# Layer 2 of a four-layer mixture kernel: the next batch's first two up products moved ahead of this batch's last down product, and two DVE steps moved by one or more slots

## What is computed

```python
# conditioning: y = x @ W_base.T + b_base + low-rank expert part (rank 16 of each of 8 experts)
out = einsum('btc,oc->bto', x, W_base) + b_base
h = einsum('btc,erc->bter', x, As)
y = out + einsum('bter,eor,be->bto', h, Bs, w) * SCALING
# feed-forward on the better half of the tokens (k = 256 of 512), F = 1024
scores = einsum('bsd,d->bs', y, w_router)
top_scores, top_idx = top_k(scores, k)
weights = sigmoid(top_scores)
h = gelu(selected @ W1 + b1)
update = weights[:, :, None] * (h @ W2 + b2)      # added to the selected tokens, the others pass through
x = x + (y + scattered update)
```

## Time and profile before

| | |
|---|---|
| median of three executions | 1460.94 us |
| the profiled execution, its own time | 1467.98 us |
| its span, first to last instruction | 1465.3 us |
| PE busy | 1292.0 us, 88% of the span |
| DVE busy | 1017.1 us, 69% |
| POOL busy | 628.9 us, 43% |
| ACT busy | 573.3 us, 39% |
| mean granted TensorE clock | 0.926 of full speed |
| layer 2 from up(1, 0) to the last down product | 698.34 to 800.60 us of the span |

### The profile page before, as it was taken

One profiled execution on the slowest core, in us unless ns is written; L12 is line 12 of the kernel. 1 busy time (PEld: TensorE's weight loads), 2 busy tenths in 40 slices (PEclk: granted clock), 3 DMA queues, 4 the chain that ended last, 5 costly groups with the idle time before them and its releaser, 6 DMA issues.

```text
span 1465.3 us, 18770 instructions
## 1 busy us (share of the span) xinstructions
PE 1292.0 (88%) x6536; PEld 1093.1 (75%) x6536; DVE 1017.1 (69%) x1854; ACT 573.3 (39%) x960; POOL 628.9 (43%) x339
## 2 busy tenths in 40 slices
PE   5998999998992899838888999999899989996798
PEld 4898687897791799826677787877678777875687
DVE  8699777599662555546766433489748994799986
ACT  3401423303320688714445454434443344432242
POOL 4320115620015567573303462375445442565691
PEclk9899999899975899969999999999899999998799
DMA  6310002310007689851101647323213161232000
GB/s 193 145 37 15 29 19 82 132 29 1 0 15 254 206 274 315 264 172 43 44 0 35 223 169 250 127 73 126 111 50 109 50 244 65 73 122 101 0 1 29
DMA packets 45885, 154.96 MB, mean 106 GB/s; under 512 B 6992, under 2 KB 7776, under 8 KB 45664
## 3 DMA queue, kind: packets, MB, share of 16 engines
q1 hardware_dynamic: 38848, 136.08, 27.7%
q0 software_dynamic: 4608, 12.59, 2.6%
q10 hardware_dynamic: 2336, 5.11, 0.9%
HBM read 120.98 MB, written 32.77 MB: 105 GB/s over the span
## 4 chain that ended last, share of the span: by engine, by line
PE 57%; DVE 22%; issue 9%; POOL 5%; ACT 4%; DMA 2%; SPq 1%; DVEq 0%; ACTq 0%; POOLq 0%
PE bank L442 17%; PE bank L446 16%; PE bank L445 16%; DVE G L498 3%; DVE bank L2472 3%; DVE acc L2496 2%; DVE F L2496 2%; POOL w_lo L679 1%; POOL VW L498 1%; PE bank L1056 1%; PE bank L1228 1%; POOL xs L687 1%; PE bank L1373 1%; DVE acc L2628 1%; PE bank L928 1%
## 5 line engine op out<-in xcount | busy, mean ns | idle before, releaser
L442 PE MATMUL bank<-x_hi,w_hi 128*128 128x512 f32 (+1 forms) x560 | 218.6, 390 | 27.9 <-POOL w_lo L725 6.3
L445 PE MATMUL bank<-x_lo,w_hi 128*128 128x512 f32 (+1 forms) x560 | 212.6, 380 | 0.0
L446 PE MATMUL bank<-x_hi,w_lo 128*128 128x512 f32 (+1 forms) x560 | 212.2, 379 | 0.0
L725 POOL TENSOR_TENSOR w_lo<-raw,w_hi 128x1024 fp32r<-128x1024 f32 x36 | 89.4, 2482 | 196.1 <-ACT w_hi L1718 181.9
L442 PE MATMUL bank<-hid_hi,w_hi 128*128 128x512 f32 x328 | 133.3, 406 | 22.6 <-DVE hid_lo L2427 12.3
L442 PEld LDWEIGHTS bank<-x_hi,w_hi 128*128 128x128 f32 x560 | 110.2, 197 | 54.5 <-issue 18.5
L1819 ACT ACTIVATE hid_hi<-bank 128x512 fp32r<-128x512 f32 x96 | 57.6, 600 | 215.1 <-DVE bank L2472 215.1
L445 PE MATMUL bank<-hid_lo,w_hi 128*128 128x512 f32 x328 | 131.2, 400 | 0.0
L446 PE MATMUL bank<-hid_hi,w_lo 128*128 128x512 f32 x328 | 130.8, 399 | 0.0
L446 PEld LDWEIGHTS bank<-x_hi,w_lo 128*128 128x128 f32 x560 | 109.7, 196 | 19.2
L445 PEld LDWEIGHTS bank<-x_lo,w_hi 128*128 128x128 f32 x560 | 110.2, 197 | 17.8
(11 more groups left out here) (468 smaller groups left out, 3537.1 us busy)
## 6 DMA issues: line engine op xcount, KB each, us to landing
raw<-in_skill SPq DMA_DIRECT2D x32, 768.0 KB
raw<-in_l1e SPq DMA_DIRECT2D x20, 513.0 KB
base<-xs SPq DMA_DIRECT2D x38, 256.0 KB, 4.4
ys<-F SPq DMA_DIRECT2D x38, 256.0 KB, 4.8
VW<-in_l1e SPq DMA_DIRECT2D x18, 513.0 KB, 5.3
w_hi<-kept SPq DMA_DIRECT2D x12, 768.0 KB, 4.3
w_lo<-kept SPq DMA_DIRECT2D x12, 768.0 KB, 6.1
raw<-in_l0c SPq DMA_DIRECT2D x12, 512.0 KB
```

Source lines behind the costliest of these rows:

```text
L442: i = nc.tensor.matmul(out, sh, mh, start=first, stop=False)
L445: nc.tensor.matmul(out, sh, ml, start=False, stop=False)
L446: return nc.tensor.matmul(out, sl, mh, start=False, stop=last)
L725: nc.gpsimd.tensor_tensor(lo[:, UP3], src[:, UP3], hi[:, UP3].bitcast(F32), ALU.subtract).then_inc(w_up_ready.sem, 1)
```

## The change

On PE, up(b + 1, 0) and up(b + 1, 1) leave the head of the next batch: the first is issued ahead of `weights_of_tokens(b)`, the second between it and down(b, 7). On DVE, `add_ffn(b - 1)` moves from m = 0 to m = 1, and the four rank steps from m = 0, 1, 2, 3 to m = 0, 2, 3, 4. `x2_residue(b + 1)` stays at m = 4 and now stands ahead of a rank step. ACT, POOL and SP have the same instructions in the same order.

```diff
             for b in range(BATCH):
                 for m in range(8):
-                    l2_up(b, m)
+                    if b == 0 or m >= 2:
+                        l2_up(b, m)
                     if m >= 1:
                         l2_down(b, m - 1)
...
+                if b + 1 < BATCH:
+                    l2_up(b + 1, 0)
                 weights_of_tokens(b)
+                if b + 1 < BATCH:
+                    l2_up(b + 1, 1)
                 l2_down(b, 7)
...
+            RANK_SLOT = [0, 2, 3, 4]
             for b in range(BATCH):
                 u = b % 2
                 for m in range(8):
...
-                    if m == 0 and b > 0:
+                    if m == 1 and b > 0:
                         add_ffn(b - 1)
                     if m == 3 and b + 1 < BATCH:
                         add_experts(b + 1)
-                    if m < NT:
-                        rank_tokens(b, m)
+                    if m == 4 and b + 1 < BATCH:
+                        x2_residue(b + 1)
+                    if m in RANK_SLOT:
+                        rank_tokens(b, RANK_SLOT.index(m))
                     if m == 4:
-                        if b + 1 < BATCH:
-                            x2_residue(b + 1)
                         select_tokens(b)
```

## The result

| | before | after |
|---|---|---|
| median, five executions each | 1460.05 us | 1448.77 us |
| lowest and highest | 1458.51, 1464.66 | 1445.28, 1452.40 |
| the profiled execution, own time | 1467.98 us | 1452.24 us |
| its span | 1465.3 us | 1449.8 us |

The sign was right, the size was not. The execution behind the rows ahead of the prediction, 1467.98 us, is none of the five timed ones and lies above them all; the profiled one of after, 1452.24, is among its five. That will matter.

A forecast was written before the change was run, and what follows sets the result against it. PE, busy 88% of the span, was taken to bound the kernel, so only its idle time could pay. Batches 1, 2 and 3 gave 0 + 2.35 + 2.6 = 5.0 us: 1460.94 - 5.0 = 1456.0 us, range 1451.5 to 1460.5.

The forecast's parts named there:

- Batch 2: Layer 2, batch 2: gaps ahead of down(2, 0) and down(2, 1) go, transposes then wait for add_ffn(1); gives 2.35 us.
- 1.00 granted: Batch 2, PE's clock: no fall behind the 2.51 us gap, cited against the rival of a slower kernel.
- Batch 3: Layer 2, batch 3: down(3, 1) 3.4 us earlier, full clock, less a new collision; gives 2.5 to 2.6 us.
- the collision: Batch 3, slice 2: DVE's rank step 1 meets POOL's x_lo and stalls 1.9 us; without it batch 3 gives 4.2.
- batch 1 gives nothing: Layer 2, batch 1: PE's signal waits for gathers to land, so gelu of slice 3 stays at about 712.5; 0 us.
- Batch 1 gives too: Rival, chance 0.27: batch 1's late signal is fixed in length or moves with PE; 2.35 more, 7.3 us in all, 1453.6.
- Most is lost: Rival, chance 0.15: larger collision in batch 3, clock falls behind batch 1's new wait; 1 to 3 us remain, about 1459.
- Slower by the clock: Rival, chance 0.06: clock falls at new waits and layer 3's start cost 8 us against 5; about 1463.

The follow-up runs named there:

- before_paced: The kernel before, with POOL waiting after every three gathers of batches 2 and 3 until these have landed; ratio 0.9977 to the kernel before, 1458.37 us.
- before_third: The kernel before, unchanged, run again on a chip where it took 1467.58 us; ratio 1.0006.
- before_fourth: The kernel before, unchanged, run again on a chip where it took 1469.58 us; ratio 0.9977.
- before_again: The kernel before, unchanged, profiled a second time on a chip where it took 1468.59 us; ratio 0.9992.
- after_again: The changed kernel, unchanged, profiled a second time; ratio 0.9942 to the kernel before, which took 1468.59 us on that chip.
- after_fourth: The changed kernel, unchanged, on a chip where the kernel before took 1467.58 us; ratio 0.9926 to the kernel before.
- paced: The changed kernel, with POOL waiting after every three gathers of batches 2 and 3 until these have landed; ratio 0.9907 to the kernel before, 1446.47 us.
- paced_again: The changed kernel with gathers of batches 2 and 3 issued three at a time, on a chip where the kernel before took 1467.58 us; ratio 0.9910.
- all_together: The changed kernel plus gathers in threes, ACT's later rounding, and rank steps at slices 1, 2, 2, 4 (batch 0: 0, 2, 2, 4); 0.9848 of before, 1449.46 us.

## Why the prediction was wrong, step by step

**Batch 2, right in mechanism, 0.1 to 0.2 off.** Forecast: up(2, 0) 2.28 us earlier, and the copy of the weights as the gate of gelu of slice 0, 0.74 earlier. Measured, against the scores' copy: 2.28 and 0.91 (the gelu follows the start of the copy by 0.49, not 0.66). No gap ahead of down(2, 0) and down(2, 1), 1.04 ahead of the transposes for 1.1, and the transposes 2.54 earlier for 2.35. What the term left out is the clock. The first profile showed no fall in batch 2, and I wrote "1.00 granted" as evidence against. For batch 2 it was the exception: five profiles of kernels with a gap there show the fall, and in the four with the order of before batch 2 is 1.3 to 1.6 longer. The change removes gap and fall, which makes its gain 3.8 to 4.1. So the clock in batch 2 was put at nothing on the strength of one execution.

**Batch 3, mis-sized: 3.2 for 2.6.** down(3, 1) came 3.6 earlier (3.4 forecast), down(3, 2) after 0.41 us of idle time (0.5), the clock stayed at 1.00, and the collision happened at the place named. It cost 1.62 us (1.90 for 0.28) against the 1.9 taken, so the selection was ready 0.43 us before its forecast time, and ACT's table load (19.46 us behind the scores' copy, 22.68 before) started another 0.29 before the selection ended, since it doesn't wait for it. In three other profiles with the order of before (before_paced, before_third, before_fourth) batch 3 takes 32.3 instead of 31.9, and against these the gain is 3.6; there the fall began within 0.3 us of the end of the gap, and in the two with 31.9 it began 0.4 and 1.0 us behind it. The Trainium skill (SBUF — State Buffer, "Who interferes with whom") says that the loser waits for the whole of the other; DVE's instruction started 0.63 us after POOL's 2.38 and ended 0.15 after it, which agrees.

**The failing step: "batch 1 gives nothing", 0 for 2.5 us.** The mechanism that I read out of one profile is real, and the runs confirm it: PE's signals are held until the gathers have landed, or nearly, and where that happens batch 1 stays at 36.6 to 36.8 with and without the change. But it doesn't happen everywhere. In the two profiles of the change where the kernel before takes 1460, nothing is held, and batch 1 takes 33.2 to 33.3; for the kernel before without the hold, before_paced gives 35.7. There the first rival ("Batch 1 gives too") is what came about, at 2.5 us, though not for the reasons it gave.

I took a stall out of an execution that isn't one of those whose median I forecast. The profiled execution lay 7.04 us above the median and above all of the timed ones, and I moved the sum to the median as if the two differed in nothing that the change touches. It has the held signals and only 47 of the 192 records, as the profiles on the chips where this kernel takes 1468 to 1471 have; the profiles on the chip with 1460 have neither. That it came from such a chip is likely and not on record. A long time alone is no sign of the hold: before_third has it at 1457.06 us, the shortest of its ten executions. (A small slip besides: I gave the delay in batch 1 as 1.2 us, which is 1.0 by the measure that gives 3.3 in batch 0.)

**The sums.** Held, in the layer: 6.4 us (before_again to after_again: -0.8, 0.0, 4.0 and 3.2 by batch) and 7.4 (before_third to after_fourth: 0.3, -0.3, 3.8 and 3.6). Not held, paced: 10.2. Of the 5.2 us that the forecast's 5.0 lacks there, 2.5 are batch 1, 1.7 batch 2 (mostly the clock) and 1.0 batch 3. The measured medians are apart by 11.3 in the first result, by 11.4 on the chip without the hold (11.9 between the paced kernels), and by 8.3 and 8.2 on the two with it: 0.8 to 1.8 us more than the layer in each of the three pairs with profiles, and what makes these isn't known. Batch 0 varies from 31.0 to 38.3 by execution; with paced gathers it is 34.22 with and without the change, so none of that can be put down to the change.

**The other rivals.** "Most is lost" and "Slower by the clock" didn't come: in batch 1 of after_fourth PE does stand 2.78 us ahead of down(1, 3), as the first said, and the granted clock over that batch is 0.95; but the 1.37 us that stand ahead of down(1, 4) in before_third are gone, as it also said, and the batch is 36.83 for 36.57. In after_again the same wait, 2.80 us, brought no fall, and batch 1 is 36.59. The sum of the second is 1463.9 by its own numbers (8 us against 5), not about 1463. The clock is at 1.00 through batches 1 to 3 of after. The Trainium skill advises against idle gaps between matmuls (TensorE: Matmul & The Clock Gate, "Why this matters for your kernels"); the 0.57 to 0.64 behind batch 2's gap points the same way, and belonged on the side of a larger gain, while the equal gap of batch 1 had no fall.

**Left open.** Why signals are held in some executions and not in others is not known; it goes with the chip and with lost records, and no run separates the two. That pauses between the gathers remove the hold rests on two paced profiles, paced_again and all_together. The kernel before was never profiled unpaced in an execution without the hold, so that its batch 1 is 35.7 there rests on before_paced alone.

## What to carry to other kernels

When the profiled execution isn't among those whose median you forecast, take no stall in it as given: here the stall that decided a term was in the profile and not behind the median. One more profile on the chip that gave the times would have shown it. A gap between matmuls is worth its length and, in some executions, the slow matmuls behind it (9 of 15 cases here), so price its removal with a range over both. And a producer's "I'm done" can be late though its work isn't: compare the consumer's start with the end of the producer's last instruction, not with its wait.

## What the hardware showed that I had not expected

- Behind a run of gathers without a pause, increments of PE's semaphores arrived up to 6.2 us late, the last of them together at the end of the gathers; with a pause behind every three, none did. On three chips every unpaced profile has it (twelve in all); on a fourth the one unpaced profile hasn't; of the first two profiles, before has it and after hasn't.
- The same profiles lack most records of the gathers' own increments (39 to 74 of 192 are there for batch 3), and those without the hold where the kernel before takes 1460 have nearly all (189 to 192).
- Equal gaps (2.48 to 2.53 us) in the same place of a batch were followed by a fall of the clock in none of five profiles in batch 1, in four of five in batch 2 (0.57 to 0.64 granted) and in five of five in batch 3.
- ACT's operation behind the copy of the weights starts 0.49 us after the copy did, though the copy is shown with 0.60.
